# The feed-forward matmuls moved to the last steps of a batch in a differential-attention kernel

## The reference, cut to what matters

```python
qkv = hidden_states @ Wqkv_w.T + Wqkv_b
q = q.reshape(B, S, H // 2, 2, D)
p = p1 - lam * p2                      # two causal softmax maps per head pair
o = jnp.einsum('bhqk,bkhe->bqhe', p, v)
rms = jax.lax.rsqrt(jnp.mean(o * o, axis=-1, keepdims=True) + EPS)
o = o * rms * subln_w
...
    xn = _layernorm(x, axis=-1)
    s = _L0_attn_ref(xn, ...)
    g = _silu(_L0_ffn_ref(xn, L0_ffn_weight, L0_ffn_bias))
    x = x + s * g
```

## Time and profile before

| what | us |
|---|---|
| median of 3 runs | 1755.01 (1752.3 to 1758.83) |
| the profiled execution: its own time | 1754.4 |
| its span in the trace | 1752.6 |
| busy in the span: TensorE | 1538.7 (88%) |
| VectorE | 1196.0 (68%) |
| ScalarE | 885.8 (51%) |
| GpSimd | 662.4 (38%) |

### The profile page before, as it was taken

How to read it: one execution, slowest core, us unless ns; L and a number is a source line. 1 busy time by engine, 2 the same in 40 slices (tenths; PEclk the granted TensorE clock), 3 DMA queues, 4 the chain that set the end, 5 groups by cost and what they waited for, 6 DMA issues and landing times. The chain is left out here.

```text
span 1752.6 us, 28521 instructions
## 1 busy us (share of the span) xinstructions
PE 1538.7 (88%) x9137; PEld 899.8 (51%) x9153; DVE 1196.0 (68%) x3177; ACT 885.8 (51%) x2542; POOL 662.4 (38%) x1161
## 2 busy tenths in 40 slices
PE   2666588999989988999889988999989989899898
PEld 1343355555555555545555555545555546555554
DVE  4467777776777677776677667775777767675682
ACT  4563356535663456535664356634564356533561
POOL 2103542345324443344424443244424443243433
PEclk7778799999999999999999999999999999999999
DMA  7401334333342334333352334324342333422433
GB/s 250 140 4 27 64 67 82 61 88 70 50 91 55 84 73 82 64 78 72 55 87 57 84 73 79 68 46 100 55 85 54 95 63 65 80 54 67 64 76 73
DMA packets 385353, 130.63 MB, mean 75 GB/s; under 512 B 366354, under 2 KB 366900, under 8 KB 385204
## 3 DMA queue, kind: packets, MB, share of 16 engines
q1 hardware_dynamic: 385204, 128.81, 35.4%
HBM read 31.74 MB, written 8.39 MB: 23 GB/s over the span
## 5 line engine op out<-in xcount | busy, mean ns | idle before, releaser
L690 ACT ACTIVATE ph<-ps,small 128x128 f16<-128x128 f32 (+3 forms) x256 | 134.4, 525 | 395.0 <-DVE ps L981 394.4
L1168 POOL TENSOR_SCALAR norm<-psum_l,small 128x1 f32<-128x1 f32 x256 | 88.4, 345 | 584.9 <-ACT pp L681 584.9
L970 DVE CUSTOM_DVE_ANT_0 ps<-ps,mask,ssc 128x384 f32<-128x384 f32 (+3 forms) x512 | 279.7, 551 | 35.9 <-PE ps L547 35.4
L490 PE MATMUL ps<-xT,wqkv 128*128 128x512 f16 x768 | 297.6, 387 | 6.8 <-DVE qkv L940 6.4
L491 PE MATMUL ps<-xT,wqkv 128*128 128x512 f16 x768 | 296.4, 386 | 0.0
L492 PE MATMUL ps<-xT,wqkv 128*128 128x512 f16 x768 | 295.5, 385 | 0.0
L940 DVE SCALAR_TENSOR_TENSOR qkv<-ps,bsc,qkv 128x512 f16<-128x512 f32 x192 | 143.3, 750 | 187.0 <-ACT qkv L658 187.0
L490 PE MATMUL ps<-qkv,pT 128*128 128x256 f16 x640 | 179.6, 281 | 74.3 <-DMA pT<-ph 73.5
L545 PE MATMUL ps<-qkv 128*128 128x384 f16 (+3 forms) x512 | 155.2, 309 | 56.5 <-DVE ph L987 53.6
L490 PE MATMUL ps<-wout,heads 128*128 128x512 f16 x512 | 194.1, 379 | 0.5 <-DVE small L956 0.5
L491 PE MATMUL ps<-wout,heads 128*128 128x512 f16 x512 | 194.0, 379 | 0.0
(11 more groups left out here) (147 smaller groups left out, 3146.9 us busy)
## 6 DMA issues: line engine op xcount, KB each, us to landing
xin<-in_L_attn_hidden_states SPq DMA_DIRECT2D x8, 1024.0 KB, 5.8
xres<-in_L_attn_hidden_states SPq DMA_DIRECT2D x32, 256.0 KB, 2.8
out_x<-res SPq DMA_DIRECT2D x32, 256.0 KB, 2.4
qkv<-in_L_attn_Wqkv_w SPq DMA_DIRECT2D x8, 512.0 KB, 7.3
heads<-in_L_attn_Wqkv_w SPq DMA_DIRECT2D x8, 512.0 KB, 10.7
pT<-ph SPq DMA_TRANSPOSE x256, 2.7
heads<-on SPq DMA_TRANSPOSE x256, 2.5
qkv<-in_L_attn_out_w SPq DMA_DIRECT2D x4, 512.0 KB, 5.6
```

Source lines behind the costliest of these rows:

```text
L490: mm(out, ah, bh, start=start and j == 0, stop=False)
L690: run(ph[:, n % PH, 0:w], sc_ps[u][:, 1, 0:w], ACT.Copy, scale=sigma).then_inc(ph_hi, 1)
L970: nc.vector.tensor_tensor_reduce(sc, sc, mask[:, S - w:S], ssc[:, c:c + 1], BIG, ALU.add, ALU.min, ebias[:, u, m:m + 1]).then_inc(max_done, 1)
```

## The change

`FFN_STEP` puts the four feed-forward fills of a batch in steps 22 to 25 instead of 10 to 13. The two V projections that were in steps 15 and 16 go to 14 and 15. The x split happens in iterations 14, 16, 18 and 19 instead of 15, 17, 18 and 19, and its halves lie in `gate`, which is idle between the last output fill and the new place of the feed-forward fills, instead of in `res`, `xres` and `aq`. The quantised input keeps its transposes in `xres` and `res` from steps 10 and 11 on (before: 9 and 10). VectorE's drain of a feed-forward fill gets a wait for the transpose of that tile of x. The output of the squares goes to the free half of the PSUM bank that they read, and the identity matrix of the setup to a spare place. In the last batch the load of the first residual moves from step 22 to 25. `PH` has the same value as before.

```diff
-PH = 4 - AHEAD
+PH = 2
...
-FFN_STEP = 10
+FFN_STEP = 22
...
     for g in (1, 2, 3):
 
-        at = (None, PROJ_AT, PROJ_AT[:6] + (7, 8), (0, 1, 1, 2, 3, 3, 4, 5))[g]
+        at = (None, PROJ_AT, PROJ_AT, (0, 1, 1, 2, 3, 3, 4, 5))[g]
         for s, (kind, j) in zip(at, PROJ):
             steps[(g - 1) * STEPS + s].append((kind, g, j))
...
-X_SPLIT = {15: 0, 17: 1, 18: 2, 19: 3}
+X_SPLIT = {14: 0, 16: 1, 18: 2, 19: 3}
...
-        junk = sb("junk", [P, E], BF16)
...
-        ident = sb("ident", [P, P], F32)
...
-        xh = [t[:].bitcast(F16).rearrange("p (s h) -> p s h", s=2) for t in (res, xres)]
-        xh += [aq[:, 2 * u:2 * u + 2, :].bitcast(F16) for u in range(2)]
+        xh = [gate[:, k, :].bitcast(F16).rearrange("p (s h) -> p s h", s=2) for k in range(NT)]
...
+        ident = spare[:, 256:384]
...
+        junk = [ps[:, 6, E:2 * E], ps[:, 7, E:2 * E]]
...
+            for k in range(NT):
+                sp.wait_ge(xT_done[k], 16)
             sp.dma_start(gate[:], fw_d.rearrange("(k p) h -> p k h", p=P)).then_inc(ld_fw, 16)
...
                 if s == 0 and b:
-                    sp.wait_ge(xT_done[1], 16 * (b + 1))
                     residual(b - 1, 0)
...
-                if b == B - 1 and s == LAST_STEP:
+                if b == B - 1 and s == FFN_STEP + 3:
+                    sp.wait_ge(fill_done, fill_of("ffn", b, 0, 1) + 1)
                     residual(b, 0)
-                for k in {FFN_STEP - 1: (0, 1), FFN_STEP: (2, 3)}.get(s, ()):
+                for k in {10: (0, 1), 11: (2, 3)}.get(s, ()):
...
-                run(junk[:], o_ps[n % 2], ACT.Square, scale=SQ_SCALE, accum_out=sumsq[:, n % 2:n % 2 + 1])\
+                run(junk[n % 2], o_ps[n % 2], ACT.Square, scale=SQ_SCALE, accum_out=sumsq[:, n % 2:n % 2 + 1])\
...
                 if n % NT == 0 and n:
                     act.wait_ge(res_free, 16 + 16 * (n - NT))
-                    act.wait_ge(q_done, 2 * NT)
+                    act.wait_ge(wT_done, 16 * NT)
...
                     wait(dve, gated, f.gate - NT + 1)
+                    if f.gate // NT + 1 < B:
+                        dve.wait_ge(xT_done[j], 16 * (f.gate // NT + 2))
                     tt(gate[:, j, :], bank, fbias[:], ALU.add).then_inc(fill_free, 1)
```

More of the change, by code:

```diff
@@ L588, in _ @@
                 for c in range(4):
-                    last = tr(setup_bank(m)[:, c * P:(c + 1) * P], slot(kind, n // 2)[:, n % 2, c * P:(c + 1) * P], ident[:])
+                    last = tr(setup_bank(m)[:, c * P:(c + 1) * P], slot(kind, n // 2)[:, n % 2, c * P:(c + 1) * P], ident)
                 last.then_inc(su_pe, 1)
@@ L1077, in _ @@
             pt = nc.gpsimd.tensor_tensor
-            for m in (ident, mask):
-                nc.gpsimd.memset(m[:], 0.0).then_inc(consts, 1)
+            for m in (ident, mask[:]):
+                nc.gpsimd.memset(m, 0.0).then_inc(consts, 1)
             pool.wait_ge(consts, 2)
             for m in (ident,):
-                nc.gpsimd.affine_select(out=m[:], in_=m[:], compare_op=ALU.not_equal, fill=1.0, base=0,
+                nc.gpsimd.affine_select(out=m, in_=m, compare_op=ALU.not_equal, fill=1.0, base=0,
                                         pattern=[[-1, P]], channel_multiplier=1).then_inc(consts, 1)
```

## The result

The changed kernel takes 1762.43 us (median of 7 runs, 1761.58 to 1764.47), the kernel before, on the same chip, 1756.58 (7 runs, 1752.3 to 1759.75). The ratio is 1.0036, with a 95% interval of 1.0026 to 1.0047: slower, by less than the 0.5% that the prediction calls no change. The forecast was 1759.

The account below looks back on a forecast made before the run. Idle TensorE waits for probabilities in steps 14, 22 and 23, and a ScalarE-GpSimd gating loop bound the kernel. Gain and loss of 7.3 us cancel in seven batches; +3 and +2 for half clock on 1754.4 give 1759, range 1738 to 1780.

Parts of the forecast that it names:

- The loop: Feed-forward fills tie ScalarE's exponential and tanh to GpSimd's gating; one turn in steps 12 to 15 took 6.8 us before.
- Gain 7.3 us a batch in steps 8 to 16: Feed-forward fills gone and V moved up: 7.9 us less 0.3 and 0.3 in charges, between 6.0 and 8.4.
- likeness: Steps 24 to 31 and next step 0, with the same fills and widths, used to price the changed steps 8 to 16.
- Turns 1 to 3: Iterations 23 to 27: two turns between second exponentials, 6.2 and 7.9 us, then 7.4 to step 27's low half of probabilities.
- Loss 7.3 a batch: Steps 22 to 27: low half of step 27's probabilities ends at 913.9 instead of 906.6; bounds 5.0 and 9.0 us.
- The start of the loop: Iteration 23's second exponential at 891.29, delayed by the first fill's tanh, taken at 1.1 us, to 892.4.
- Last batch: Short steps without k show the loop in full: a loss of 9.7 us for a gain of 7.3.
- The sum: Seven batches at 0, first 0.5 less gain, last 2.4: +3; half clock +2; from 1754.4 that is 1759 us.
- Parts at no cost: `PH`, the squares' output place, identity, feed-forward weights' load and the drain's wait for transposed x: put at nothing.
- The half clock: Slower rival: unhidden half clock behind two new gaps, 1.7 to 3.4 us a batch, 1771 to 1783 us; chance 0.2.
- The faster rival: The loop does not close in the short steps 22 to 25; a batch wins 4.2 us, time 1721; chance 0.12.
- the rival: V moved up gains less: x split delays probabilities of steps 16 and 17, 2 us lost, 1775 us; chance 0.1.

## Why the prediction was right

The forecast was two large terms of one size, and so they are. The loop came out turn by turn; two terms that were put at nothing were not nothing, and part of the match of the sums is luck. By its own steps:

- **Gain 7.3 us a batch in steps 8 to 16.** 48.9 - 41.5 = 7.4 over batches 2 to 6, "41 to 42 us" as foreseen, and the clock is 1.00 in steps 14 and 15. The likeness of steps 24 to 32 was the right kind of price, but the match is partly luck. By the same averages steps 24 to 32 took 42.0 us before, 6.9 less than steps 8 to 16 and not 7.9, and the changed kernel takes 0.5 less than its likeness, where 0.6 more was charged: steps 10 to 13 are 0.3 and step 16 is 0.5 longer, but step 8 is 0.6 and steps 14 and 15 are 0.7 shorter than the steps they were likened to.
- **Turns 1 to 3.** From second exponential to second exponential: 892.65 - 886.56 = 6.1 (6.2 foreseen), 900.49 - 892.65 = 7.8 (7.9); then to the end of the low half of the probabilities at 907.36 + 0.48 = 907.8, 7.4 (7.4). These three are the same to 0.01 us in all of the batches 0 to 6:

```profile
907.36 0.48 DVE L990 SCALAR_TENSOR_TENSOR ph<-ps,small,ph 128x256 f16<-128x256 f32 x1
```

- **Loss 7.3 a batch.** 56.35 - 48.70 = 7.65. The start of the loop was oversized in batch 3: the second exponential of iteration 23 comes 7.3 us after the start of step 22, 0.6 later than before, where 1.1 was taken. So the low half ends 28.6 us after that start instead of 29.3 (22.0 before). What this saves is lost again in part in steps 28, 29 and 31, which are 0.2 us longer each on average. In batches 4 to 6 the start is another 0.6 to 1.2 us later (see the parts at no cost).
- **TensorE's waits.** 3.5 us in step 25, for k 0's bank, where some 4 were foreseen. In step 27 it waits 0.78 us for the probabilities, not 2.5; in batch 1 the same loop shows as 2.7 us in step 25 and 2.0 in step 27. TensorE is busy for 6.2 us in step 25 of batch 3, at a clock of 0.83, and for 4.5 in batch 1, at 1.00. Yet steps 22 to 27 take 33.1 us in both, so the half clock was hidden as the prediction had it.
- **Missed: step 18, 0.96 us a batch.** The prediction followed the x split only into iteration 14. The second tile's moved from 17 to 16, where VectorE's low half of k stands in front of it and the combine of step 18 behind; the low half of k 1 then comes late for the q projection that needs its bank (the gap of 0.79 above). With the 0.5 us of step 16 this is some 1.4 us a batch where 0.3 was charged. The runs with other splits show that moving the tiles again wins nothing: the loss goes to another step.
- **Last batch.** The start came 1.1 us later (here the prediction took 1.2, in the loop above 1.1). The two turns took 6.1 and 6.2 (6.2 and 6.3 foreseen), the stretch to the end of the low half 5.3 (5.3). From step 22 on the batch loses 11.1 us instead of 9.7, and wins 7.9 before instead of 7.3: 3.2 longer, 2.4 foreseen.
- **The sum.** In the profiled executions the six batches 1 to 6 take 6.2 us more, the last 3.2, the first 0.1: 9.5 where 3 and 2 for half clock were foreseen. The two terms put at nothing would alone add 0.96 x 7 = 6.7 for step 18 and 2.8 for the late starts in batches 4 to 6. Against them stand the hidden half clock, the start of the other batches and the first batch, which won 7.7 and lost 6.7. That the forecast came within 4 us of the measured median is thus partly luck. The execution profiled before was faster than its median of 7 runs (1754.4 against 1756.6) and the one profiled after slower (1763.9 against 1762.4), which is why the medians differ by 5.9 only.
- **Parts at no cost.** The squares' place is shown to be nothing. The identity and the setup's wait were not tried apart. The drain's wait for the transposed x is met in batch 3, but not everywhere. VectorE in batch 4, at the first feed-forward fill:

```profile
1084.62 0.69 DVE L955 TENSOR_TENSOR gate<-ps,fbias 128x512 f32<-128x512 f32 x1 [1.06 <-DMA xT<-gate]
```

It waits 1.06 us there and 0.54 in batch 6. In batches 4 to 6 the transpose of the probabilities of step 22 too takes 4.5 to 4.8 us from issue to landing, against 3.1 to 3.3 in the batches before them and in all batches 0 to 6 of the kernel before, and TensorE is idle for 2.1 to 2.4 us in step 22 instead of 0.7 to 0.9. The loop starts 0.6 to 1.2 us later there, 2.8 us in all. Why these transposes are late was not followed.

**The rivals.** The half clock moves but doesn't grow: the mean clock of the profiled execution is 0.952 before and 0.959 after. Batch 3 has a clock of 0.83 in step 25 and 1.00 in 14, 15 and 22 to 24, where before it had 0.72 and 0.92; other batches keep some in 22 to 24 (0.76 in step 24 of batch 0). The faster rival, a loop that doesn't close, was wrong for the changed kernel, but its 1721 is nearly what the kernel takes once the loop is opened (1718). The x split did cut V's gain, by 0.5 us in step 16 and 0.96 in step 18 where the rival had 2 in steps 16 and 17. For the slow split of the first tile the prediction drew on the trace and on the Trainium skill ("SBUF — State Buffer", the part on the engines' ports). The timelines of VectorE and GpSimd in batch 3:

```profile
844.67 1.24 DVE L1010 SCALAR_TENSOR_TENSOR gate<-xin,gate 128x512 f16<-128x512 f32 x1 [1.22 <-ACT gate L712]
...
854.10 0.68 DVE L1010 SCALAR_TENSOR_TENSOR gate<-xin,gate 128x512 f16<-128x512 f32 x1
```

```profile
844.20 1.16 POOL L1141 TENSOR_TENSOR qkv<-v,qkv 128x512 f16<-128x512 f32 x1 [0.75 <-ACT qkv L664]
```

The first tile's split takes 1.24 us beside GpSimd's low half of V, the second 0.68 with GpSimd idle. This agrees with the rule, by which VectorE with two SBUF inputs waits for the whole instruction of a GpSimd that came first: GpSimd's ends at 845.36, and the split 0.55 us later.

**Best version.** The changed kernel with three tanh buffers and its own x split, 1717.8 us, is 2.1% faster than the kernel before and 2.5% faster than the changed one.

## What to carry to other kernels

When work is moved into gaps, ask first what it ties together: four small fills a batch cost 45 us in eight batches here, 5.6 us a batch, by one shared buffer between ScalarE and GpSimd, while their matmuls are 3.6 us a batch. Read such a loop by laying two engines' timelines side by side, since the releaser named may be another engine or "issue". Two moves can add up to less or more than their parts (11 and 30 us slower alone, 6 together), so test them apart, and look at a batch or a stretch that lacks one of the suspects: the last batch, without an x split, is what tells the split's share from the gating's. A gap that a small edit removes need not be a gain: here the loss went to the next steps.

## What had not been expected of the hardware

- The same gap costs more or less by the clock behind it. With V moved alone TensorE is idle for 2.9 us in step 17 of each of the batches 0 to 6, behind 1.3 to 1.4 us in step 16, and the step takes 9.2 us where the clock stays at 1.00 (batches 5 and 6), 10.5 to 10.9 at 0.84 (batches 0, 1, 2 and 4) and 12.1 at 0.72 (batch 3). In the changed kernel the gap of 2.5 us in step 23 leaves a clock of 1.00 in step 24 of batch 3, where step 23 takes 5.4 us; in batch 1 the same gap (2.6 us idle) stands in a step 23 of 6.7 us, with TensorE busy for 4.1 instead of 2.8.
- The place and type of the squares' output change 2 ns of the square (379 to 381 ns) and 14 ns of reading its sum (192 to 206 ns), though PSUM f32 and SBUF bf16 differ in size and memory.
